# A perceiver layer stack on one Trainium2 core: the first cross attention starts with a fixed block of keys

## The reference, cut to what matters

```python
mask = logical_not(arange(4096) < lenS2)       # lenS2 is drawn in 3072..4096
xn   = layernorm(x) * gamma + beta             # 256 x 256
q    = xn @ Wq                                 # 16 heads of 64
k, v = split(ctx @ Wkv)                        # ctx is 4096 x 192
dots = where(mask, q @ k.T / 8, -inf)
x    = x + softmax(dots) @ v @ Wo + bo
```

## Time and profile before

| | us |
|---|---|
| median of three runs (447.03 to 450.56) | 447.14 |
| the profiled execution, its own time | 448.73 |
| its span, first to last instruction | 446.9 |
| TensorE busy | 423.9 (95%) |
| VectorE busy | 263.5 (59%) |
| ScalarE busy | 168.8 (38%) |

### The profile page before, as it was taken

How to read it: one execution, slowest core, us unless ns; L and a number is a source line. 1 busy time by engine, 2 the same in 40 slices (tenths; PEclk the granted TensorE clock), 3 DMA queues, 4 the chain that set the end, 5 groups by cost and what they waited for, 6 DMA issues and landing times.

```text
span 446.9 us, 8130 instructions
## 1 busy us (share of the span) xinstructions
PE 423.9 (95%) x3087; PEld 305.4 (68%) x3087; DVE 263.5 (59%) x892; ACT 168.8 (38%) x429; POOL 2.5 (1%) x10
## 2 busy tenths in 40 slices
PE   6989999999999999788999999999999998989997
PEld 5645554554555789666768799988757767877774
DVE  6255554776768657787499899231436554464433
ACT  3265556656666217774413310000333323242110
POOL 1000000000000000000000000000000000000000
PEclk9999999999999999999999999999999999998999
DMA  8500010000029184000199300049292000000000
GB/s 282 171 1 1 1 47 1 1 2 1 0 80 350 51 277 194 1 1 1 41 352 324 103 3 3 1 157 220 68 394 65 0 1 0 1 2 0 0 1 24
DMA packets 24518, 36.07 MB, mean 81 GB/s; under 512 B 1694, under 2 KB 20768, under 8 KB 23968
## 3 DMA queue, kind: packets, MB, share of 16 engines
q1 hardware_dynamic: 24192, 35.48, 24.6%
q10 hardware_dynamic: 288, 0.07, 0.1%
HBM read 35.29 MB, written 0.26 MB: 80 GB/s over the span
## 4 chain that ended last, share of the span: by engine, by line
PE 46%; issue 41%; DVE 10%; ACT 1%; DMA 1%; POOL 0%; POOLq 0%; DVEq 0%; SPq 0%
PE bank L925 6%; PE bank L1149 6%; PE bank L916 6%; PE bank L1019 5%; PE bank L994 3%; PE bank L999 2%; PE bank L1163 2%; PE bank L1008 2%; DVE region_a L1774 2%; PE bank L890 1%; PE bank L1167 1%; DVE region_a L1771 1%; PE bank L771 1%; PE bank L706 1%; PE bank L970 1%
## 5 line engine op out<-in xcount | busy, mean ns | idle before, releaser
L1224 ACT ACTIVATE region_g<-bank,nm_new 128x384 f32<-128x384 f32 (+1 forms) x64 | 40.1, 633 | 32.4 <-DVE nm_new L1530 20.0
L1522 DVE CUSTOM_DVE_ANT_0 bank<-bank,bias_h 128x384 f32<-128x384 f32 (+1 forms) x64 | 38.7, 646 | 11.3 <-issue 11.2
L585 PEld LDWEIGHTS bank<-ident,region_g 128*128 128x128 f32 x226 | 24.1, 141 | 22.8 <-issue 9.0
L585 PE MATMUL bank<-ident,region_g 128*128 128x128 f32 x226 | 32.2, 281 | 1.9 <-ACT region_g L1224 1.2
L622 PE MATMUL bank<-region_a,qT 64*128 64x384 f32 (+1 forms) x128 | 32.6, 567 | 0.5 <-ACT region_g L1224 0.3
L925 PE MATMUL bank<-region_u,region_g 128*128 128x256 f32 x128 | 29.3, 383 | 0.0
L605 PE MATMUL bank<-region_d,region_a 128*64 128x256 f32 x232 | 28.6, 386 | 0.0
L890 PE MATMUL bank<-xnT,region_d 128*128 128x256 f32 x128 | 28.0, 379 | 0.0
L1210 ACT COPY region_d<-bank 128x512 f32<-128x512 f32 (+1 forms) x48 | 24.2, 538 | 9.9 <-PE bank L585 9.9
L1149 PE MATMUL bank<-xnT,region_u 128*128 128x256 f32 (+1 forms) x112 | 27.2, 402 | 0.0
L890 PEld LDWEIGHTS bank<-xnT,region_d 128*128 128x128 f32 x128 | 24.2, 190 | 3.7 <-issue 0.5
(11 more groups left out here) (354 smaller groups left out, 758.8 us busy)
## 6 DMA issues: line engine op xcount, KB each, us to landing
region_d<-in_downT SPq DMA_DIRECT2D x2, 2048.0 KB, 11.0
region_u<-in_up SPq DMA_DIRECT2D x2, 2048.0 KB, 11.6
region_a<-in_ctx SPq DMA_DIRECT2D x1, 3072.0 KB, 15.9
region_d<-in_ctxT SPq DMA_DIRECT2D x1, 2048.0 KB, 9.7
region_d<-in_ctxT SPq DMA_DIRECT2D x2, 1024.0 KB, 16.0
region_u<-in_wg SPq DMA_DIRECT2D x1, 1728.0 KB, 7.4
region_u<-in_wu SPq DMA_DIRECT2D x1, 1728.0 KB, 11.8
region_a<-in_wd SPq DMA_DIRECT2D x1, 1664.0 KB, 15.4
```

What stands on the lines that cost most here:

```text
L585: mm = nc.tensor.transpose(bank[4 + e][:, k * P:(k + 1) * P], prob[:, u % 2, e, k * P:(k + 1) * P], ident[:, :])
L1224: nc.scalar.activation(prob[:, u % 2, e, 0:tiles * P], bank[2 * s + e][:, 0:tiles * P], ACT.Exp, scale=-1.0, bias=nm_new[:, p, t, e:e + 1] ...
L1522: ins = nc.vector.tensor_tensor_reduce(bank[2 * s + e][:, 0:size], bank[2 * s + e][:, 0:size], bias_h[:, t, 0:size], -1.0, 3e38, ALU.add, ...
```

## The change

The first block no longer depends on the mask. It is the last 384 keys (`TAIL` = 3712 on), loaded right after `x`. The range search works on the rest: a group's end is cut at the tail, the number of turns is counted from the same limits less the 6 groups of the tail, and the bytes of the mask's tail are set to zero once the first block has used them, so that a block of the loop which reaches into the tail counts nothing twice. For any given mask of the reference's kind the number of turns is what it was.

On the engines:

- SyncE's order is now `x`, the block of keys, the first half of `Wkv`, `Wq`, the mask in two parts (first the tail's 384 bytes of each row, then the rest), the second half of `Wkv`, and the small ones. It reads the range later, just before the load of the loop's first block.
- TensorE makes the first two units of keys and values, then four query products, the scores of head 0 tile 0, the other four query products, and goes on. The 8 extra transposes are gone. The count over the tokens comes in head 3 (`COUNT_AT`), and the `value_load` at the entry to the loop.
- VectorE has the two reductions of `find_blocks` behind heads 0 and 1, `find_range` ahead of the maxima of head 4, and the three small operations ahead of those of head 5. Its two `value_load`s are at the entry to the loop.
- ScalarE copies three of the four pairs of query products before the first exponentials and the fourth between them, and has its `value_load` at the entry to the loop.

```diff
--- before.py
+++ after.py
...
+SPARE = 15
+COUNT_AT = 3
...
+TAIL = S2 - FIRST * P
...
             sp.dma_start(x_res[:, :, :], a["x"].rearrange("(t p) d -> p t d", p=P)).then_inc(x_in, 16)
-            for t in range(TT):
-                sp.dma_start(mask_w.bitcast(U32)[:, t, 0:S2 // 4], a["mask"][t * P:(t + 1) * P]).then_inc(mask_in[t], 16)
-            for t, (lo, hi) in enumerate(((0, 2 * P), (2 * P, 8 * P))):
-                sp.dma_start(wq[:, :, lo:hi], a["Wq"].rearrange("(c p) n -> p c n", p=P)[:, :, lo:hi]).then_inc(wq_in[t], 16)
-            sp.dma_start(blk_ends[:, :], a["block_ends"]).then_inc(small_in, 16)
...
-            load_wkv(0, wkv_in)
-            sp.wait_ge(range_set, 1)
-            first = sp.value_load(rng_i[0:1, 0:1], min_val=0, max_val=GROUPS - 1)
...
-            load_block(within(first * GRP, S2 - GRP), FIRST)
+            load_block(TAIL, FIRST)
+            load_wkv(0, wkv_in)
+            for t, (lo, hi) in enumerate(((0, 2 * P), (2 * P, 8 * P))):
+                sp.dma_start(wq[:, :, lo:hi], a["Wq"].rearrange("(c p) n -> p c n", p=P)[:, :, lo:hi]).then_inc(wq_in[t], 16)
+            for t, (lo, hi) in enumerate(((TAIL // 4, S2 // 4), (0, TAIL // 4))):
+                sp.dma_start(mask_w.bitcast(U32)[:, :, lo:hi], a["mask"].rearrange("(t p) n -> p t n", p=P)[:, :, lo:hi]
+                             ).then_inc(mask_in[t], 16)
             load_wkv(1, wkv_rest_in)
-            n_turns = sp.value_load(rng_i[0:1, 1:2], min_val=1, max_val=NTURN)
+            sp.dma_start(blk_ends[:, :], a["block_ends"]).then_inc(small_in, 16)
             sp.dma_start(pick_pair, a["pick_pair"].rearrange("p (j n) -> p j n", j=2)).then_inc(pick_in, 16)
             sp.dma_start(rows[:, :], a["rows"].partition_broadcast(P)).then_inc(rows_in, 16)
+            sp.wait_ge(range_set, 1)
+            first = sp.value_load(rng_i[0:1, 0:1], min_val=0, max_val=GROUPS - 1)
+            n_turns = sp.value_load(rng_i[0:1, 1:2], min_val=1, max_val=NTURN)
             sp.wait_ge(kv_psum, XP)
-            load_block(within(first * GRP + FIRST * P, S2 - GRP + FIRST * P), KT_PER)
+            load_block(within(first * GRP, S2 - BLK), KT_PER)
             with sp.Fori(0, n_turns) as i:
                 sp.wait_ge(kv_psum, i * XP + 2 * XP)
-                load_block(within(first * GRP + FIRST * P + (i + 1) * BLK, S2 + PAD - BLK), KT_PER)
+                load_block(within(first * GRP + (i + 1) * BLK, S2 + PAD - BLK), KT_PER)
...
-            turn_xn(pe, 1, (bank[0], bank[1]), spare=15)
-            for k in range(8):
-                nc.tensor.transpose(bank[3][:, k % 4 * P:(k % 4 + 1) * P], ident[:, :], ident[:, :])
-            pe.wait_ge(wq_in[0], 16)
...
-            for m in range(8):
-                if m == 2:
...
-                if m == 0:
-                    pe.wait_ge(blocks_seen, 1)
-                    for t in range(TT):
-                        mm = nc.tensor.matmul(bank[2][0:1, 0:GROUPS], lhsT=ones[:, 0:1], rhs=seen[:, t, :],
-                                              start=t == 0, stop=t == TT - 1)
-                    mm.then_inc(blocks_counted, 1)
...
-            pe.wait_ge(wkv_in, 48)
-            pe.wait_ge(blocks_counted, 1)
-            pe.wait_ge(range_set, 1)
-            n_turns = pe.value_load(rng_i[0:1, 1:2], min_val=1, max_val=NTURN)
+            def queries(tiles):
+                for m in tiles:
...
+                    for c in range(DC):
...
+                        mm.then_inc(q_psum, 1)
...
+            for k in range(SPARE):
+                nc.tensor.transpose(bank[7][:, k % 4 * P:(k % 4 + 1) * P], ident[:, :], ident[:, :])
+            turn_xn(pe, 1, (bank[6], bank[7]))
             pe.wait_ge(ctx_landed, 16)
+            pe.wait_ge(wkv_in, 48)
             keys_and_values(0, FIRST)
-            pe.wait_ge(q_ready, 4)
             keys_and_values(1, FIRST)
+            pe.wait_ge(wq_in[0], 16)
+            pe.wait_ge(xnT_ready, 2)
+            queries((0, 1))
+            pe.wait_ge(wq_in[1], 16)
+            queries((2, 3))
+            pe.wait_ge(q_ready, 1)
...
             for p in range(XP):
                 scores(p, 0, FIRST, 0, 0)
+                if p == 0:
+                    queries((4, 5, 6, 7))
+                if p == 1:
+                    pe.wait_ge(q_ready, 4)
+                if p == COUNT_AT:
+                    pe.wait_ge(blocks_seen, 1)
+                    for t in range(TT):
+                        mm = nc.tensor.matmul(bank[7][0:1, T:T + GROUPS], lhsT=ones[:, 0:1], rhs=seen[:, t, :],
+                                              start=t == 0, stop=t == TT - 1)
+                    mm.then_inc(blocks_counted, 1)
                 if p == XP - 1:
                     first_values(p - 2)
                 if p >= 1:
@@ -642,12 +647,16 @@
                 if 2 <= p < XP - 1:
                     first_values(p - 2)
                 scores(p, 1, FIRST, 0, 0)
+                if p == 0:
+                    pe.wait_ge(q_ready, 2)
                 turn(p, 0, FIRST, 0, 0)
                 if p + 2 == KT_PER:
                     pe.wait_ge(wkv_rest_in, 48)
                 if p + 2 < XP:
                     keys_and_values(p + 2, FIRST)
             pe.wait_ge(pads_set, 4)
+            pe.wait_ge(range_set, 1)
+            n_turns = pe.value_load(rng_i[0:1, 1:2], min_val=1, max_val=NTURN)
...
-            for j in range(4):
+            def copy_queries(j):
                 act.wait_ge(q_psum, j + 1)
                 nc.scalar.activation(qT[:, 2 * j:2 * j + 2, :], bank[4 + j][:, :].rearrange("p (m q) -> p m q", m=2),
                                      ACT.Copy, scale=XD ** -0.5).then_inc(q_ready, 1)
-
-            act.wait_ge(range_set, 1)
-            n_turns = act.value_load(rng_i[0:1, 1:2], min_val=1, max_val=NTURN)
...
             copy_keys(0, FIRST, 0)
             copy_keys(1, FIRST, 0)
+            for j in range(3):
+                copy_queries(j)
             act.wait_ge(pads_set, 4)
...
                 if p < XP - 1:
                     exps(p, 0, FIRST, 0, 0, sums)
+                if p == 0:
+                    copy_queries(3)
                 exps(p, 1, FIRST, 0, 0, sums)
                 turned_half(p, 0, 0, FIRST, 0)
                 if p + 2 < XP:
                     copy_keys(p + 2, FIRST, 0)
+            act.wait_ge(range_set, 1)
+            n_turns = act.value_load(rng_i[0:1, 1:2], min_val=1, max_val=NTURN)
...
-            nc.vector.memset(mask_w[:, :, S2 // 4:], 0.0)
...
+            def find_blocks(t):
+                dve.wait_ge(mask_in[1], 16)
+                ins = nc.vector.tensor_reduce(seen[:, t, :],
+                                              mask_w.bitcast(U32)[:, t, 0:S2 // 4].rearrange("p (g w) -> p g w", g=GROUPS),
+                                              AX.X, ALU.max)
+                if t == TT - 1:
+                    step(ins)
+                    nc.vector.tensor_scalar(seen[:, :, :], seen[:, :, :], 1.0, None, ALU.min).then_inc(blocks_seen, 1)
+                    step(nc.vector.memset(mask_w[:, :, TAIL // 4:S2 // 4], 0.0))
...
                 step(nc.vector.scalar_tensor_tensor(ends.rearrange("p (k b) -> p k b", k=2),
-                                                    bank[2][0:1, 0:GROUPS].unsqueeze(1).to_broadcast([1, 2, GROUPS]), 1.0,
+                                                    bank[7][0:1, T:T + GROUPS].unsqueeze(1).to_broadcast([1, 2, GROUPS]), 1.0,
...
-            find_blocks()
-            find_range()
-            step(nc.vector.tensor_reduce(any_q[:, :], seen[:, :, :], AX.X, ALU.max))
-            step(nc.vector.reciprocal(is_row[:, :], any_q[:, :]))
-            step(nc.vector.tensor_tensor(is_row[:, :], is_row[:, :], any_q[:, :], ALU.mult))
-
-            dve.wait_ge(range_set, 1)
-            first = dve.value_load(rng_i[0:1, 0:1], min_val=0, max_val=GROUPS - 1)
-            n_turns = dve.value_load(rng_i[0:1, 1:2], min_val=1, max_val=NTURN)
...
-            set_bias(within(first * GRP, S2 - GRP), FIRST, 1)
             copy_values(0, FIRST, 0)
             copy_values(1, FIRST, 0)
+            dve.wait_ge(mask_in[0], 16)
+            set_bias(TAIL, FIRST, 1)
             for p in range(XP):
+                if p == COUNT_AT + 1:
+                    find_range()
+                if p == COUNT_AT + 2:
+                    step(nc.vector.tensor_reduce(any_q[:, :], seen[:, :, :], AX.X, ALU.max))
+                    step(nc.vector.reciprocal(is_row[:, :], any_q[:, :]))
+                    step(nc.vector.tensor_tensor(is_row[:, :], is_row[:, :], any_q[:, :], ALU.mult))
                 maxima(p, 0, FIRST, 0, nm_new).then_inc(nm_ready, 1)
...
                 turned_half(p, FIRST, 0)
                 if p + 2 < XP:
                     copy_values(p + 2, FIRST, 0)
+                if p < TT:
+                    find_blocks(p)
             dve.wait_ge(nm_ready, 2 * XP)
             keep_maxima(1)
+            dve.wait_ge(range_set, 1)
```

(8 more changed lines are left out.)

24 lines of the change are left out of this document (6 added, 18 removed).

## The result

The changed kernel takes **451.16 us** in the median (22 runs), the kernel before 449.40 us on the same chips (22 runs). The ratio is 1.0052, 95% interval [1.0036, 1.0069], so 1.6 to 3.1 us slower. Predicted was no change, 447.3 against 447.14. The difference is within 1%, but 451.16 lies outside the range of 445.2 to 449.3, and the interval excludes no change.

The account below looks back on a forecast made before the run. TensorE, busy for 95% of the span, was taken to bound the kernel. The terms -3.0 + 1.2 + 0.3 + 0.9 + 0.8 = +0.2 gave 448.9 against the profiled 448.73, carried over to 447.3 us; range 445.2 to 449.3.

Parts of the forecast that it names:

- The start: From kernel start to first scores of head 1: these come at 24.85 in place of 27.84, 3.0 us earlier.
- So 7.8, and 7.9 for the first matmul: Landing of the first half of Wkv at 7.8 us, TensorE's first unit at 7.9; bounds 7.5 and 8.6.
- Rival 4: At the start, TensorE's clock falls after waiting for weights; 6 us more, 453 us. Chance 0.02.
- The sum of the parts: First unit to first scores of head 1: 5.2 + 6.9 + 1.8 + 0.7 + 2.35 us.
- First reduction: find_blocks' first reduction on VectorE, ahead of the maxima of head 1, where there is no slack: +1.2 us.
- second: find_blocks' second reduction with clipping and clearing, ahead of head 2's maxima: 0, or 1.7 us without cover.
- count: Four short matmuls in head 3 on a TensorE without idle time: +0.3 us.
- `find_range`: VectorE's 1.67 us of single steps ahead of head 4's maxima, slack 0.8: +0.9 us, bounds 0.6 and 1.7.
- the rows without keys: Three VectorE operations for empty rows ahead of head 5, 0.65 us against slack of 0.8: 0.
- `value_load`: TensorE's load at the entry to the loop, with nothing queued to hide it: +0.8 us, bounds 0.4 and 0.9.
- Rival 2: Heads catch up, so search is mostly free and only count and load stay: 444.4 to 446.2 us. Chance 0.22.
- rival 3: Heads 2, 4 and 5 have no slack, so VectorE work delays transposes: 448.8 to 451.2 us. Chance 0.14.

Follow-up runs that it names:

- packed and held back: The changed kernel with the first half of Wkv as one packed transfer and nothing issued behind it until it landed: ratio 0.9984 to the kernel before.
- the packed kernel: The changed kernel with the first half of Wkv as one transfer of 128 rows of 6 KB, in place of three: ratio 0.9978 to the kernel before.
- held back: The changed kernel with SyncE waiting for the first half of Wkv to land before issuing Wq, the mask and the rest: ratio 1.0012 to the kernel before.
- range early: The changed kernel with both reductions ahead of head 0's maxima and count and find_range in head 0: ratio 1.0065 to the kernel before.
- spare transposes: The changed kernel with 20 spare transposes of the unit matrix before TensorE's wait for the first weights: ratio 1.0014 to the kernel before.

## Why the prediction was wrong

**The start, -3.0: the step that failed**, with +2.0 measured. Its parts:

- *"So 7.8, and 7.9 for the first matmul"*: 10.66 and 9.85. I took 344 KB/us from the mask and `Wq`, which come in pieces of 4 and 3 KB, for a block in pieces of 1.5 KB and weights in pieces of 2 KB at the head of the queue. (2048 KB in 6.0 us is 341; that changes nothing.) I had seen that the 64-row parts of the same weights fell behind the rate, counted 0.4 for it, and set the upper bound at 8.6. Packing and holding back, together, gave 8.05, and packed alone the weights were once in by 7.15. The number was reachable, not with these transfers. How the 2.76 us divide between the size of the pieces and the volume issued behind them stays open: held back, packing was worth 0.9 us (7.9 against 8.8); in 2 KB pieces holding back was worth 0.9 to 1.8, in packed form nothing clear of the scatter.
- *Rival 4, the clock*: I gave it 0.02, since the wait "is 0.4 us, as long as the one at 8.4 before". The argument hung on the wait being short, and so on the first error: with 2.79 us of standing still the unit ran at 1.2 GHz. The price that I set, 6 us over two units and four products, was too high as well; it is 1.6, over the first unit. The Trainium skill (TensorE: Matmul & The Clock Gate, What's actually happening) has an idling TensorE set back to 1.2 GHz. The change's row with 0.50 agrees. In the packed kernel the durations agree as well (1.92 us for two matmuls in place of 1.02) and the record, at 1.00, does not.
- *The sum of the parts*: 17.54 from first unit to first scores of head 1 in the run with the forecast's start, where I had 16.95. The eight products took 7.3 and not 6.9 (the row of 6.31 us for seven gives 7.2), the two units 5.5 and not 5.2 (the second one took its full 2.76 here, where 2.45 had passed before the scores began). 0.6 us.

Together 2.76 + 1.6 + 0.6 is the 5.0 of the first row.

**The steps behind it held.** First reduction +1.02 (1.2; moving it gave -1.0), second 0, count +0.32 (0.3), `find_range` +0.76 (0.9; moving it gave -0.4 net), the rows without keys 0, `value_load` +0.93 (0.8; moving it gave -0.9). Rival 2 (the search is mostly free) and rival 3 (no slack) fall: the losses are kept, but not one of them grew.

**The part behind the entry** was to move as a whole. It doesn't quite: the iota table gives back 1.4 us.

**The base.** The absolute forecast stood on 447.14, the median of three runs, and 1.6 us were taken off the profiled execution for it. Over 22 runs the kernel before has 449.40: even with the change forecast rightly at +0.2 the time would have been 449.6, outside the range.

The measured difference is 2.3 [1.6 to 3.1]. The rows give 5.04 - 1.4 = 3.6 us from one pair of profiles, above that interval, and 2.8 with the means of both pairs (loop at 75.12 and 70.87), within it. The range failed by the base, and because it took the bounds of the landing (7.5 to 8.6) as far as nearby rows went and gave the clock no part in the case of a late landing: these two errors come together.

## What to carry to other kernels

Before work is put first that needs a transfer, read the rate from transfers with pieces of the same size: from 4 to 6 us pieces of 1.5 and 2 KB moved 208 to 278 GB/s, those of 3 to 6 KB 320 to 422. A wait at the start can cost more than its length if it is TensorE that stands still: 1.5 us and more behind waits of 1.05 to 2.8 us, nothing behind 0.36 and 0.91. Spare matmuls in the wait gave that back up to the loop; that the whole kernel gains by them no ratio here shows. Take the base from as many runs as the comparison will have: three were 2.3 us off. And cover has to be counted at both ends: the search cost next to nothing beside the query products, and 2.1 us among the heads, although VectorE was busy there for only 3.76 of 7.11 us.

## What the runs showed of the hardware

- Behind 1.05 to 1.2 us of standing still TensorE ran the next unit in 4.25 to 4.56 us in place of 2.7 while the granted clock read 1.00 throughout (packed, held back), and behind 2.29 us in 5.26 (range early). Behind 0.91 and 0.36 us it ran at full speed (spare transposes, packed and held back).
- TensorE's granted clock falls for about 3 us in some executions, at different places, for 1.0 to 1.7 us each. In the two profiles of before TensorE was busy for 2.47 and 2.41 of the 3 us ahead of 403, once with the fall and once without.
- At a DMA share of 0.9 to 1.0 the queue moved 249 packets with 0.42 MB in 2 us in small pieces, 250 packets with 0.80 MB in large ones.
- The packed weights landed 5.4, 6.4 and 7.2 us after issue with other transfers behind them, and 6.2 us with none, about 1.6 us after the DMA share had fallen below 0.2.
- The same 64 KB load took 1.7 to 1.9 us to land in nine profiles and 3.0 to 3.5 in five. In the kernel before it was long both times, in the change short both times.
